# Graph attention layer: GpSimd copies the index columns of its gathers once per chunk instead of once per gather

## The reference, cut to what matters

```python
def reference(x, src, dst, ...):           # x: 3125 x 256, 50000 edges, dst sorted
    xn = _layernorm(x)
    # graph attention, 8 heads of 32: for each edge e = (src, dst)
    #   sim = q[dst] . k[src] * scale, softmax over the edges of one dst,
    #   agg[dst] = sum attn * v[src]
    x = x + _L0_gnn_ref(xn, edges, ...) + _L0_mix_ref(xn, ...)[0]
    x = x + _L0_ffn_ref(_layernorm(x), ...)    # 8 experts, 489 rows each
    return x
```

## Time and profile before

| | |
|---|---|
| median of 3 runs | 1285.04 us (1282.04 to 1286.11) |
| the profiled execution | 1296.26 us, span 1294.5 us |
| gathers of line 888 | 408, the first starts at 255.7 us, the last at 903.2 us |
| busy in the span | PE 976.9, DVE 875.1, POOL 655.0, ACT 475.0 us |

### The profile page before, as it was taken

How to read it: one execution, slowest core, us unless ns; L and a number is a source line. 1 busy time by engine, 2 the same in 40 slices (tenths; PEclk the granted TensorE clock), 3 DMA queues, 4 the chain that set the end, 5 groups by cost and what they waited for, 6 DMA issues and landing times. The chain is left out here.

```text
span 1294.5 us, 18792 instructions
## 1 busy us (share of the span) xinstructions
PE 976.9 (75%) x4183; PEld 679.3 (52%) x4184; DVE 875.1 (68%) x1736; ACT 475.0 (37%) x1294; POOL 655.0 (51%) x1037
## 2 busy tenths in 40 slices
PE   0899655677777777778677777776688379999996
PEld 0455342455555554545455454554457346666664
DVE  2678655887888797888888788897775313344433
ACT  2466324533443353334434443443425112211220
POOL 0515273577777677777777777776000022222221
PEclk9999867787778787877888787888796569999998
DMA  4243172167667666766676676666023433233320
GB/s 155 88 104 87 52 205 73 41 182 206 178 176 199 177 186 174 204 187 186 177 204 182 177 195 190 191 184 188 4 75 121 175 100 110 93 116 113 114 94 7
DMA packets 82666, 183.55 MB, mean 142 GB/s; under 512 B 11862, under 2 KB 46476, under 8 KB 82629
## 3 DMA queue, kind: packets, MB, share of 16 engines
q0 software_dynamic: 39488, 126.26, 36.0%
q1 hardware_dynamic: 40297, 54.53, 12.8%
q10 hardware_dynamic: 2844, 2.35, 0.6%
HBM read 166.03 MB, written 20.85 MB: 144 GB/s over the span
## 5 line engine op out<-in xcount | busy, mean ns | idle before, releaser
L888 POOL DMA_INDIRECT slot<-kv_d,idx x408 | 401.0, 983 | 177.1 <-issue 72.6
L1129 PE MATMUL at_pa<-at_pv,at_hot 128*125 128x264 f32 x880 | 292.5, 478 | 121.7 <-DVE agg L1010 110.5
L1129 PEld LDWEIGHTS at_pa<-at_pv,at_hot 128*125 128x125 f32 x880 | 190.0, 233 | 200.4 <-DVE agg L1010 104.8
L1119 PE MATMUL at_pq<-q,at_hotT 125*128 x1320 | 192.0, 309 | 11.5 <-POOL at_sign L874 6.7
L980 DVE TENSOR_TENSOR at_prod<-at_pq,slot 128x1024 f32<-128x1024 f32 x110 | 133.8, 1216 | 66.0 <-DMA slot<-kv_d,idx 55.1
L1119 PEld LDWEIGHTS at_pq<-q,at_hotT 125*128 125x128 bf16 x1320 | 140.3, 110 | 47.6 <-issue 14.6
L996 DVE TENSOR_TENSOR at_pv<-slot,at_pp 128x1056 f32<-128x1056 f32 x110 | 136.8, 1244 | 17.4 <-issue 8.6
L914 ACT ACTIVATE at_habs<-iota_w,nloc_e 128x125 f32<-128x125 f32 x440 | 138.0, 384 | 3.4
L987 DVE TENSOR_REDUCE at_sc<-at_prod 128x32 f32<-128x1024 f32 x110 | 133.4, 1212 | 2.0
L918 ACT ACTIVATE at_hot<-at_habs,one_col 128x500 f32<-128x500 f32 x110 | 78.3, 712 | 131.4 <-PE at_pa L1129 98.5
L1570 POOL DMA_INDIRECT out<-slot,node_s x32 | 32.5, 1015 | 166.9 <-DVE slot L1603 166.9
(11 more groups left out here) (289 smaller groups left out, 1348.1 us busy)
## 6 DMA issues: line engine op xcount, KB each, us to landing
slot<-in_w SPq DMA_DIRECT2D x16, 1024.0 KB
locrow<-loc_d SPq DMA_DIRECT2D x28, 500.0 KB
slot<-kv_d,idx POOLq DMA_INDIRECT x408
kv_d<-vst SPq DMA_DIRECT2D x25, 128.9 KB
base<-in_x SPq DMA_DIRECT2D x5, 625.0 KB
kv_d<-kst SPq DMA_DIRECT2D x25, 125.0 KB
row_d<-base SPq DMA_DIRECT2D x5, 625.0 KB
out<-base SPq DMA_DIRECT2D x5, 625.0 KB
```

What stands on the lines that cost most here:

```text
L888: pool.indirect_dma_start(slot[par][:, u, :], None, m.kv_d, bass.IndirectOffsetOnAxis(ap=m.idx[:, par, u:u + 1].bitcast(U32), axis=0)).the ...
L1119: mm = pe.matmul(pq[q % 2][:, u * D:(u + 1) * D], hotT[:, 4 * q + u, :], at(m.q3, wins[u // 2])[:, part, :], start=(part == 0), stop=(part ...
L1129: mm = pe.matmul(pa[p % 2][:, 0:H * VW], hot[:, u % 8, :], pv[:, u % 8, :, :].rearrange("p h c -> p (h c)"), start=(u % 2 == 0), stop=(u % ...
```

## The change

The sixteen columns of the next chunk are copied by one operation, 128x16, after the tenth gather of a chunk (`u == 9`), in place of one 128x1 copy behind each gather. The wait for `idx_ready` stands once, ahead of the chunk's first gather, and is for the copy made in the chunk before. The wait for `pv_made` ahead of each quad stays. Ahead of the loop one copy stands for four.

```diff
-                def index(c, par, u):
-                    pool.tensor_copy(m.idx[:, par, u:u + 1], at(m.src_e, c)[:, u:u + 1]).then_inc(S.idx_ready, 1)
+                def index(c, par):
+                    pool.tensor_copy(m.idx[:, par, :], at(m.src_e, c)).then_inc(S.idx_ready, 1)
 
                 def gather(c, par, steps):
+                    pool.wait_ge(S.idx_ready, c - 1)
+                    pool.nop(nofuse=True)
                     for u in range(steps):
                         if u % 4 == 0:
-                            pool.wait_ge(S.idx_ready, U * c + u - 2 * U + 4)
-                            pool.nop(nofuse=True)
 
                             pool.wait_ge(S.pv_made, QUADS * c + u // 4 + 1 - 2 * QUADS)
                             pool.nop(nofuse=True)
                         pool.indirect_dma_start(slot[par][:, u, :], None, m.kv_d,
                                                 bass.IndirectOffsetOnAxis(ap=m.idx[:, par, u:u + 1].bitcast(U32), axis=0)).then_inc(S.arrived[par * QUADS + u // 4], 16)
-                        if u + 4 < steps:
-                            index(c, par, u + 4)
-                        elif steps == U:
-                            index(c + 1, 1 - par, u + 4 - U)
-                for u in range(4):
-                    index(2, 0, u)
+                        if u == 9 and steps == U:
+                            index(c + 1, 1 - par)
+                index(2, 0)
```

## The result

On the chip where the two kernels were first compared, the changed kernel takes 1214.2 us (median of 4, 1213.1 to 1217.7) and the kernel before 1284.5 (median of 4): ratio 0.946 [0.943, 0.948]. That is 70 us faster where 42 were forecast, outside the range.

A forecast was written before the change was run, and what follows sets the result against it. A loop of waits between DVE and POOL sets the pace, no engine full. All 25 rounds short, 25 x 23.75 = 593.8, saves 41.3 us; with about 1 from the first round, 42 off gives 1243 us; 8 in 10 for 1229 to 1267.

The forecast's parts named there:

- Spacing of the gathers: POOL's gathers: 1.27 us apart in a quad without copies, 5.15 from quad to quad; 0.2 a chunk for the new copy.
- The copies are worth little, the wait much: On POOL: a removed copy gives back 0.06 us; the wait behind the index copy leaves 0.88 idle per quad.
- POOL on time in every round, all rounds short: Every first quad's gathers start 0.76 us behind `weigh`; all 25 rounds take 23.75 us, 41.3 less than 635.06.
- rival D: First quad's fourth gather held by `turned_hots` in all 25 rounds: 26.6 us each, 30 us slower, 1315; 6 in 100.
- What is late next: DVE's own round: 21.0 us busy plus near 2 of waits for PE and ACT, 23.2; at most 55 us gained.
- The signs: In the trace: quads 5.1 to 5.2 us apart, `at_pv` wait up 60 or more, `product` row wait under 15, no alternation.
- B: POOL on time, but rows land behind `locrow`, or POOL late by tenths: long rounds 25.3 us, 1264; 2 in 10.
- C: DMA engines set when rows land, whatever POOL does: no difference, 1285 us; 1 in 10.

## Why the prediction was wrong, step by step

*Spacing of the gathers: right.* Forecast 1.27 and 5.15 a quad, measured 1.25 and 5.0. The wait for `pv_made` keeps nothing of the 0.88, and the 128x16 copy costs 0.07 of the 0.2 allowed.

*The copies are worth little, the wait much: right, and stronger than put.* The copies' share in the time is nil on the first kind (0.944 with all of them).

*POOL on time in every round, all rounds short: nearly.* Three rounds of 25 are long (27.18, 26.87 and 27.40). The last two follow on a gather in a first quad that had been held for no shown reason (1.67 us of "issue" at 647.90 in chunk 20's). Such a hold comes every 88 gathers in both kernels, 1.4 to 1.6 us in before and 0.9 to 1.7 in the changed one; in a first quad it costs 5 us. The first long round follows on a late start of chunk 3 (2.95 us of "issue" at 263.58), whose fourth gather then starts 0.14 behind `turned_hots` and takes 1.43. That is the hold of rival D, once in 25 rounds; elsewhere `turned_hots` stretches a fourth gather to 1.06, or 1.13 in chunk 2, and D did not come.

*What is late next: this step failed.* The prediction took DVE's "near 2 of waits for PE and ACT" a round as fixed, put the floor at 23.2 us a round and 55 us in all, and took a short round of before (23.75) as the size of every round. Measured: 22.71 a round, and 21.2 to 22.1 in 17 of them. The 1.04 us too much, 25 times, are 26 us, nearly all of the miss. The trace was not to blame: in the second trace of before the twelve rounds under 25 us have a mean of 23.75 too. They were short of waits for rows, but they were also the ones that follow a long wait, with the clock at 0.67 to 0.79, and so had the most waits for PE and ACT, 2.3 us each. A round of the changed kernel has 0.7 of these and 0.7 of waits for rows. The short rounds were the wrong model for a kernel without long waits. The term was also misread: in the 25 rounds of its own trace 30 us, 1.2 a round, were waits for PE and ACT, and for another 20 the trace named no cause. The clock stood in the earlier trace rows (0.78 in both short rounds, 0.82 and 0.88 in the long ones), and the text used it only as a way in which things could get worse. In sum: 50 us (25 times 2) of waits for engines were to stay, 17 did (14 in a second trace of the changed kernel). That the clock is the reason is argued, as said above; that these waits went is measured. The waits for rows that stayed, 17 us in the rounds and 19.9 in all, are a little over the 15 that were granted.

*The signs.* The idle time of POOL behind `idx` is gone from its waits and the alternation is gone, as forecast. POOL's wait for `at_pv` grew by 44 us (98.7 against 54.6), not by 60 or more, which fits rounds that are shorter than forecast; and one first quad has a gather of over 1.4 us.

*Rivals.* B would have long rounds of 25.3 and C none of the gain: neither. The DMA engines do land rows later now, 4.2 us from issue against 3.7, at a share of 0.76, but the gathers go out early enough. D forecast the slower side for a reason that did not come; the slower side came, on another chip, by another mechanism that nobody had named.

## What to carry to other kernels

A copy on GpSimd that is used at once costs its wait (0.7 us here), not its work; made a few instructions earlier it was free. When one engine's cycle is just above that of the one it feeds, removing a little less than the difference gives little, and removing the difference gives nearly all at once. Where a long wait is removed, do not model the new steady state on rounds that stood behind such waits: TensorE's clock was halved there. When a view calls a wait "remote", look up which semaphore came last: here it was TensorE's, and not the rows. And a result from one chip need not hold on the next: compare on several before a wait that spaces out DMAs is taken away.

## What the runs showed of the hardware

- PEclk went from 1.00 to 0.50 over a stretch of 5.54 us in which PE was busy for 1.25, stayed at 0.50 for some 12 us behind it, and then was at 1.00 but for one stretch of 3 us.
- 128x1, 128x4 and 128x16 copies of int32 on GpSimd all took 0.19 to 0.21 us (medians).
- Two kinds of chip, 1.5% apart for the kernel before, were 17% apart for the changed one (1213.9 and 1424.9 us).
- On the second kind of chip TensorE's signal came 0.5 us or more behind the product that gives it in 57 of 110 cases and over 5 us in 39; on the first kind none by more than 0.02.
- In ten traces a gather that starts 0.08 to 0.57 us after `turned_hots` ends 1.56 to 1.60 us after the start of `turned_hots`, so it takes up to 1.51 us in place of 0.95 to 0.97. One that starts 0.14 to 0.43 ahead of it is held too and ends 0.86 to 0.87 after that start; one from 0.1 ahead to 0.07 behind is not held.
